# A decoder layer on one core: FFN activations transposed by DMA instead of TensorE, and the tile loop unrolled

## The chip, the cores and the metric

The kernel runs on one core of a Trainium2 chip. The metric is device time in microseconds; the median of three runs of the kernel before is 566.8 us (564.99 to 567.63). Five engines work side by side and meet only at semaphores: TensorE (PE; its weight loads are shown as PEld), VectorE (DVE), ScalarE (ACT), GpSimd (POOL) and SyncE (SP), which issues the DMAs here.

## The reference

One pre-norm decoder layer on x [4, 1024, 256], in three residual parts. The first is a gated linear recurrence along the sequence; the second is cross-attention with 16 heads on 64 context rows and one null key; the third is a quantized FFN of width 1024. The change touches the third:

```python
def _act_quant(x):
    scale = 127.0 / jnp.clip(jnp.max(jnp.abs(x), axis=-1, keepdims=True), 1e-05)
    xq = jnp.clip(jnp.round(x * scale), -128.0, 127.0) / scale
    return x + jax.lax.stop_gradient(xq - x)
def _bitlinear(x, w):
    return jnp.einsum('bsi,oi->bso', _act_quant(x), _weight_quant(w))
gate = jax.nn.silu(_bitlinear(x, w_gate))
up = _bitlinear(x, w_up)
return _bitlinear(gate * up, w_down)

x = x + _L0_attn_ref(_layernorm(x), w_qkva, gamma)
x = x + _L0_xattn_ref(_layernorm(x), ctx_2048, Wq, Wkv, null_kv, Wout, ln_scale, ln_bias)
x = x + _L0_ffn_ref(_layernorm(x), w_gate, w_up, w_down)
```

So each row of activations is scaled by its own maximum and rounded to an integer twice: ahead of gate and up (256 values, here n), and ahead of the down product (1024 values, here h).

## The kernel before

The 4096 rows are T = 32 tiles of 128 rows. Stage 1, up to about 187 us, is the recurrence and the folding of the attention weights. Stages 2 and 3, attention and FFN, then run in one software pipeline over the tiles. Each engine has its own function `stages2_3(n, u4)`, called with n from -2 to 37, and in step n it works on different tiles at once: softmax of tile n+2, attention output of tile n, statistics of x2 for n-2, the FFN's input for n-3, hidden layer for n-5, and quantizing, transposing and down product for n-6. What runs when is set by the order in which these functions are written; an engine stands still at each wait. `tiles(...)` runs steps -2 to 7 and 28 to 37 as straight code and steps 8 to 27 as a hardware loop of four steps a pass. `late(n)` (n >= 32) picks another order in the last steps, where only the FFN is left.

The FFN of one tile, by lines of the kernel before. ScalarE normalizes (L670, `norm3`); VectorE takes the maximum (L1074) and makes scale and reciprocal (L1098, L1101, `qs` and `qr`). GpSimd multiplies and adds MAGIC, which rounds (L535), then subtracts it into bf16 (L542, `n3`). TensorE transposes n (L1332, `input_T`), ScalarE evicts it (L678, `nT3`). TensorE makes gate and up (L1120, `gate_up`), ScalarE applies silu (L662, after loading its table), and VectorE multiplies (L1003, `hidden_layer`) and takes the maximum (L1078). ScalarE scales h and adds MAGIC (L718); VectorE subtracts MAGIC into bf16 (L1047, `nh3`). TensorE transposes the eight blocks (L1383), ScalarE evicts them (L737, `nhT3`). TensorE makes the down product (L1120 with `wdT`), VectorE adds it (L1011, `residual`), and SP stores the tile (L431).

Of the attention: GpSimd makes p (L495, L498) from `rden` (L990, after `exp_sum`, L985). TensorE transposes p into banks 4 and 5 (L1351, L1359, and L1363 for the null part pTn). ScalarE evicts bank 4 (L709) and pTn (L712), VectorE pTn's lesser part (L1031) and bank 5 (L1036). TensorE multiplies (L1373, L1392, L1393); VectorE takes statistics (L1085, L1091); GpSimd makes scale and bias in three small instructions (L522 to L528); ScalarE applies them (L652, `norm_out`); GpSimd adds (L483 to L487). GpSimd has three like them for the FFN's norm (L509 to L515).

Of the kernel before, what the change touches and what calls it, by code (L numbers as in the profile page):

```python
# [21 lines left out]
BF16 = mybir.dt.bfloat16  # L22
ALU = mybir.AluOpType
# [9 lines left out]
def decoder_layer(nc, x, ctx_in, w_qkva, gamma, Wq, Wkv, null_kv, Wout, ln_scale, ln_bias,  # L33
# [25 lines left out]
    with ExitStack() as stack:  # L59
# [66 lines left out]
        hw = sbuf("hw", [P, 2])  # L126
# [22 lines left out]
        def carve(region, spec):  # L149
            views, at = {}, 0  # L150
            for name, n in spec:
# [12 lines left out]
                             ("nvsel", HC * NP)])  # L164
# [42 lines left out]
        nhT3 = s["nhT"].bitcast(BF16).rearrange("p (k n) -> p k n", k=FC)  # L207
# [115 lines left out]
        nT_psum = sem("nT_psum")  # L323
        nT_ready = sem("nT_ready")
# [7 lines left out]
        nhT_psum = sem("nhT_psum")  # L332
        nhT_ready = sem("nhT_ready")
# [53 lines left out]
        S23 = (-2, 8, T - 4, T + 6, 4)  # L387
# [5 lines left out]
        def _(sp):  # L393
# [42 lines left out]
        def _(pool):  # L436
# [41 lines left out]
            def stages2_3(n, u4):  # L478
# [10 lines left out]
                if exists(n + 1, T):  # L489

                    pool.wait_ge(rden_done, n + 2)
                    if positive(n):
# [8 lines left out]
                        .then_inc(p_ready, 1)  # L501
                if exists(n - 2, T):
# [27 lines left out]
                if exists(n - 3, T):  # L530
# [6 lines left out]
                    count, free = registers(pool, n - 2, n - 4)  # L537
                    pool.wait_ge(consts_set, 2)
                    pool.wait_ge(zq_done, count)
                    if positive(free):  # L540
                        pool.wait_ge(nT_psum, free)
# [3 lines left out]
            tiles(pool, stages2_3, *S23)  # L545


        @block.scalar
        def _(act):
# [123 lines left out]
            def input_T(n, u):  # L673

                act.wait_ge(nT_psum, n - 3)
                if positive(n - 5):
                    act.wait_ge(up_psum, n - 5)
                act.activation(nT3[:, u, :, :].rearrange("p k n -> p (k n)"), bank(6).bitcast(BF16)[:, 0:D],  # L678
                               ACT.Copy).then_inc(nT_ready, 1)

# [16 lines left out]
            def stages2_3(n, u4):  # L697
# [6 lines left out]
                if exists(n, T):  # L704
# [34 lines left out]
                if not late(n) and exists(n - 4, T):  # L739
                    input_T(n, u)  # L740
# [6 lines left out]

            tiles(act, stages2_3, *S23)


        @block.vector
        def _(dve):
# [240 lines left out]
            def hidden_layer(n, v):  # L993
# [4 lines left out]
                if late(n):  # L998
                    dve.wait_ge(nh_ready, n - 6)
                    dve.wait_ge(p_ready, 2 * T)  # L1000
                elif positive(n - 5):
                    dve.wait_ge(nh_ready, n - 5)
# [4 lines left out]
            def residual(n, slot):  # L1007
# [3 lines left out]
                dve.scalar_tensor_tensor(out=xs[:, n, :], in0=bank(5, D), scalar=hw[:, slot:slot + 1],  # L1011
# [3 lines left out]
            def stages2_3(n, u4):  # L1015
# [11 lines left out]
                if exists(n, T):  # L1027
# [5 lines left out]
                    dve.wait_ge(pT1_psum, n + 1)  # L1033
# [15 lines left out]
                if late(n):  # L1049
                    residual(n - 7, v)  # L1050
# [383 lines left out]
```

## Time and profile before

| | before |
|---|---|
| median of 3 runs | 566.8 us |
| lowest, highest | 564.99, 567.63 us |
| profiled execution: span | 562.9 us |
| median less that span | 3.9 us |
| busy PE, DVE, ACT, POOL | 512.4, 479.9, 349.1, 301.1 us |

The span runs from the first to the last instruction of the execution that was profiled; its own device time isn't listed apart, so sums are made against the span and 3.9 us are added. A row of an engine in order of time gives start, duration, engine, line and operation; a difference of two starts tells more than a duration, since instructions overlap at their ends. A bracket at a row's end is the time that the engine stood idle before it, and what it waited for.

### The profile page before, as it was taken

Reading aid. Unit: us, or ns where it says so; the run is one execution under the profiler, and the core shown is the slowest. Engines: PE = TensorE matmul, PEld = TensorE weight load, DVE = VectorE, ACT = ScalarE, POOL = GpSimd, SP = SyncE. Lnnn points to the kernel's source line nnn. Section 1 sums busy time; section 2 is a strip of 40 time slices with the busy share of each in tenths; the row PEclk is TensorE's granted clock in tenths of the full one; section 3 lists DMA queues with packets and bytes.
Section 4 is the critical chain, followed back from the end, with each engine's and each line's share of the span. In section 5 each row is a group of like instructions: output and inputs, shape, how many; then the busy total and the mean of one; then the engine's idle time right before and its main releaser. Section 6 shows DMA issues by size and latency. Waiting matters only on the chain. (4 is left out here: it accounts for less than half of the span.)

```text
span 562.9 us, 11113 instructions
## 1 busy us (share of the span) xinstructions
PE 512.4 (91%) x3226; PEld 419.2 (74%) x3226; DVE 479.9 (85%) x1017; ACT 349.1 (62%) x476; POOL 301.1 (53%) x451
## 2 busy tenths in 40 slices
PE   2889999998998888999999999999999999998765
PEld 1667778765787787888788888888887888885533
DVE  5899998969535767799999999999999999997884
ACT  4422341432142323578988888889889888885764
POOL 3112216500000467787777867776878677777740
PEclk9999999999999999899999999999999999999988
DMA  8991000000000000000000000000000000000001
GB/s 283 369 394 39 1 1 0 1 1 1 0 1 0 1 2 2 0 2 20 11 10 12 19 9 9 10 18 9 9 19 9 9 9 19 9 10 15 15 19 38
DMA packets 14925, 19.80 MB, mean 35 GB/s; under 512 B 1328, under 2 KB 12848, under 8 KB 14896
## 3 DMA queue, kind: packets, MB, share of 16 engines
q1 hardware_dynamic: 14896, 19.44, 9.9%
q8 instruction: 16, 0.26, 0.2%
q14 instruction: 13, 0.11, 0.1%
HBM read 15.24 MB, written 4.19 MB: 35 GB/s over the span
## 5 line engine op out<-in xcount | busy, mean ns | idle before, releaser
L495 POOL TENSOR_TENSOR region_d<-region_d,rden 128x1024 f32<-128x1024 f32 x32 | 60.9, 1902 | 124.5 <-DVE rden L990 124.5
L1120 PE MATMUL psum<-Mhi,xT2hi 128*128 (+1 forms) x256 | 74.8, 292 | 1.9 <-DVE xT2lo L947 1.6
L1120 PE MATMUL psum<-Mlo,xT2hi 128*128 (+1 forms) x256 | 72.4, 283 | 0.0
L1120 PE MATMUL psum<-Mhi,xT2lo 128*128 (+1 forms) x256 | 72.3, 283 | 0.0
L1373 PE MATMUL psum<-VW,region_d 128*128 (+1 forms) x256 | 61.9, 385 | 6.3 <-DVE pTn L1031 6.3
L1392 PE MATMUL psum<-VW,region_d 128*128 (+1 forms) x256 | 62.9, 389 | 0.0
L1373 PEld LDWEIGHTS psum<-VW,region_d 128*128 128x128 f32 x256 | 48.4, 191 | 16.2 <-DVE pTn L1031 7.6
L973 DVE TENSOR_REDUCE mx<-psum 128x8 f32<-128x520 f32 x64 | 44.6, 697 | 8.0 <-PE psum L1120 5.9
L1392 PEld LDWEIGHTS psum<-VW,region_d 128*128 128x128 f32 x256 | 47.1, 193 | 5.4
L1120 PEld LDWEIGHTS psum<-Mhi,xT2hi 128*128 128x128 f32 x256 | 48.2, 188 | 3.0 <-issue 2.7
L1120 PEld LDWEIGHTS psum<-Mlo,xT2hi 128*128 128x128 f32 x256 | 48.3, 189 | 0.0
L1120 PEld LDWEIGHTS psum<-Mhi,xT2lo 128*128 128x128 f32 x256 | 48.2, 188 | 0.0
L976 DVE TENSOR_TENSOR region_d<-psum,mx 128x520 f32<-128x520 f32 x64 | 44.8, 700 | 2.2
L652 ACT ACTIVATE region_d<-psum,sc 128x256 f32<-128x256 f32 x32 | 17.8, 558 | 41.3 <-POOL sc L528 41.3
L461 POOL TENSOR_TENSOR pw_out<-pw_in,expo 128x8 f32<-128x8 f32 x8 | 13.1, 1643 | 51.4 <-DVE pw_in L784 51.4
L746 ACT ACTIVATE region_d<-region_d 128x1040 f32<-128x1040 f32 x32 | 34.3, 1073 | 9.5 <-DVE region_d L976 9.3
L985 DVE TENSOR_REDUCE den<-region_d 128x16 f32<-128x1040 f32 x32 | 39.3, 1228 | 0.2
L1003 DVE SCALAR_TENSOR_TENSOR region_c<-psum,zw,region_c 128x1024 f32<-128x1024 f32 x29 | 37.2, 1284 | 1.4 <-issue 0.6
L542 POOL TENSOR_SCALAR region_c<-region_d 128x256 bf16<-128x256 f32 x32 | 35.4, 1106 | 4.8 <-POOL region_d L535 0.3
L737 ACT ACTIVATE region_d<-psum 128x1024 bf16<-128x1024 bf16 x32 | 32.5, 1017 | 8.6 <-PE psum L1383 8.6
L561 ACT ACTIVATE region_a<-psum 128x1024 f32<-128x1024 f32 x8 | 8.2, 1028 | 47.4 <-PE psum L1136 47.4
L662 ACT ACTIVATE region_c<-psum,zw 128x1024 f32<-128x1024 f32 x32 | 35.6, 1113 | 2.6 <-PE psum L1120 2.3
(153 smaller groups left out, 1403.3 us busy)
## 6 DMA issues: line engine op xcount, KB each, us to landing
out_dram<-xs SPq DMA_DIRECT2D x32, 128.0 KB, 1.7
xs<-in_x_dram SPq DMA_DIRECT2D x1, 2560.0 KB, 16.4
VW<-in_L_xattn_Wkv_dram SPq DMA_DIRECT2D x1, 2048.0 KB, 17.2
region_b<-in_L_xattn_Wkv_dram SPq DMA_DIRECT2D x1, 2048.0 KB, 17.1
xs<-in_x_dram SPq DMA_DIRECT2D x3, 512.0 KB, 6.5
region_w<-in_L_ffn_w_gate_dram SPq DMA_DIRECT2D x1, 1024.0 KB, 10.1
region_w<-in_L_ffn_w_up_dram SPq DMA_DIRECT2D x1, 1024.0 KB, 12.5
region_w<-in_L_ffn_w_down_dram SPq DMA_DIRECT2D x1, 1024.0 KB, 16.8
```

The source lines that it names most:

```text
L495: pool.tensor_tensor(p2[:, v, 0:H * MK].rearrange("p (h j) -> p h j", j=MK), e[:, :, 0:MK], rden[:, v, :].unsqueeze(2).broadcast_to([P, H, ...
L542: pool.tensor_scalar(n3[:, v, :], z3[:, v, :], MAGIC, QMAX, ALU.subtract, ALU.min) \
L662: act.activation(sg3, banks(0, 2).rearrange("p b n -> p (b n)"), ACT.Silu, scale=zw[:, v, 0:1]).then_inc(silu_ready, 1)
L737: act.activation(nhT3.rearrange("p k n -> p (k n)"), bank(4).bitcast(BF16), ACT.Copy) \
L746: act.activation(e2[:, u, :], e2[:, u, :], ACT.Exp).then_inc(exp_done, 1)
L973: dve.tensor_reduce(mx[:, hh, :].rearrange("p (b h) -> p b h", h=HB), scores, AX.X, ALU.max) \
L976: dve.tensor_tensor(e2[:, u, hh * 2 * HB * J:(hh + 1) * 2 * HB * J].rearrange("p (b h j) -> p b h j", b=2, j=J), scores, mx[:, hh, :].rear ...
L985: dve.tensor_reduce(den[:, :], e2[:, slot, :].rearrange("p (h j) -> p h j", j=J), AX.X, ALU.add) \
L1003: dve.scalar_tensor_tensor(out=hidden(n - 5), in0=banks(2, 2).rearrange("p b n -> p (b n)"), scalar=zw[:, v, 1:2], in1=sg3, op0=ALU.mult, ...
L1120: mm = pe.matmul(dst, lhsT, rhs, start=i == 0, stop=i == len(terms) - 1)
L1373: pe.matmul(bank(7, D), pT[:, pair, :], VW[:, batch(n), pair, :], start=pair == 0, stop=False)
L1392: pe.matmul(bank(7, D), pT[:, pair, :], VW[:, batch(n), pair, :], start=False, stop=False)
```

## The change

1. All 39 steps, n from -2 to 38, are straight code on every engine; there is no loop in stages 2 and 3, and one step more.
2. ScalarE writes the scaled h as int16 (`nq3`, a buffer of its own), which rounds it. GpSimd casts int16 to bf16 (`nh3`, L526 of the changed kernel). VectorE's subtraction is gone.
3. GpSimd's `n3` is made by multiplying with 1 and adding -MAGIC, in place of subtract and minimum.
4. TensorE's transposes of n and h and ScalarE's two evictions are gone. SP issues two DMA transposes a tile, SBUF to SBUF: 128x1024 for h (L439) and 128x256 for n (L445), each with one semaphore for each of two destination buffers. `nhT3` has two buffers now, `nh3` and `nq3` one each. The stores of the output stand in the same queue.
5. The down product and `residual` are those of tile n-7 in every step. In steps 32 to 37 `residual` had n-7 before as well.
6. The eviction of bank 5 (pT's second half) goes from VectorE to ScalarE, ahead of the scaling of h and silu.

```diff
@@ SP
-            with sp.Fori(0, T) as t:
-                sp.wait_ge(x3_done, t + 1)
-                sp.dma_start(out_t[:, t, :], xs[:, t, :]).then_inc(stored, 16)
+            def stages2_3(n, u4):
+                u, v = u4 % 2, 1 - u4 % 2
+                if exists(n - 6, T):
+                    sp.wait_ge(nh_ready, n - 5)
+                    if positive(n - 7):
+                        sp.wait_ge(down_psum, n - 7)
+                    sp.dma_start_transpose(nhT3[u], nh3).then_inc(nhT_ready[u], 16)
+                if exists(n - 3, T):
+                    sp.wait_ge(n3_ready, n - 2)
+                    if positive(n - 4):
+                        sp.wait_ge(up_psum, n - 4)
+                    sp.dma_start_transpose(nT3[:, v, :, :], n3[:, v, :]).then_inc(nT_ready[v], 16)
+                if exists(n - 7, T):
+                    sp.wait_ge(x3_done, n - 6)
+                    sp.dma_start(out_t[:, n - 7, :], xs[:, n - 7, :]).then_inc(stored, 16)
@@ GpSimd, between p and the three small instructions
+                if exists(n - 6, T):
+                    pool.wait_ge(hq_done, n - 5)
+                    if positive(n - 6):
+                        pool.wait_ge(nhT_ready[v], 16 * ((n - 7) // 2 + 1))
+                    pool.tensor_copy(nh3, nq3).then_inc(nh_ready, 1)
...
-                    pool.tensor_scalar(n3[:, v, :], z3[:, v, :], MAGIC, QMAX, ALU.subtract, ALU.min) \
+                    pool.tensor_scalar(n3[:, v, :], z3[:, v, :], 1.0, -MAGIC, ALU.mult, ALU.add) \
@@ ScalarE
+                    act.wait_ge(pT1_psum, n + 1)
+                    act.activation(pT[:, HC // 2:HC, :], bank(5).rearrange("p (c n) -> p c n", n=P), ACT.Copy) \
+                        .then_inc(pT1_ready, 1)
...
-                    act.activation(hidden(n - 6), hidden(n - 6), ACT.Identity, bias=MAGIC, scale=qr[:, u, 0:1]) \
-                        .then_inc(hq_done, 1)
+                    if positive(n - 6):
+                        act.wait_ge(nh_ready, n - 6)
+                    act.activation(nq3, hidden(n - 6), ACT.Copy, scale=qr[:, u, 0:1]).then_inc(hq_done, 1)
...
-                if late(n) and exists(n - 4, T):
-                    input_T(n, u)
-                if exists(n - 6, T):
-                    act.wait_ge(nhT_psum, n - 5)
-                    if positive(n - 6):
-                        act.wait_ge(down_psum, n - 6)
-                    act.activation(nhT3.rearrange("p k n -> p (k n)"), bank(4).bitcast(BF16), ACT.Copy) \
-                        .then_inc(nhT_ready, 1)
@@ VectorE
-                    dve.tensor_copy(pT[:, HC // 2:HC, :], bank(5).rearrange("p (c n) -> p c n", n=P)) \
-                        .then_inc(pT1_ready, 1)
...
-                    dve.tensor_scalar(nh3, hidden(n - 6), MAGIC, QMAX, ALU.subtract, ALU.min) \
-                        .then_inc(nh_ready, 1)
                 if late(n):
-                    residual(n - 7, v)
+                    residual(n - 7)
...
-                if exists(n - 6, T) and not (isinstance(n, int) and T - 1 <= n < T + 5):
-                    residual(n - 6, u)
+                if exists(n - 7, T) and not late(n):
+                    residual(n - 7)
@@ TensorE
-                if exists(n - 6, T):
-                    pe.wait_ge(nh_ready, n - 5)
...
-                    for k in range(FC):
-                        mm = pe.transpose(bank(4).bitcast(BF16)[:, k * P:(k + 1) * P], nh3[:, k * P:(k + 1) * P],
-                                          ident16[:, :])
...
-                if exists(n - 6, T):
-                    pe.wait_ge(nhT_ready, n - 5)
+                if exists(n - 7, T):
+                    pe.wait_ge(nhT_ready[v], 16 * ((n - 7) // 2 + 1))
                     pe.wait_ge(pT1_ready, upto(n + 1, T))
-                    group(bank(5, D), [(nhT3[:, k, :], wdT[:, k, :]) for k in range(FC)]) \
+                    group(bank(5, D), [(nhT3[v][:, k, :], wdT[:, k, :]) for k in range(FC)]) \
```

TensorE's order in an odd step, from the attention product on, before; `ident` is the identity of a transpose, `VW` the attention output's weights, and region_d holds pT, n's and h's transposes:

```order
L1373 MATMUL psum<-VW,region_d 128x256 [waits pT0_ready,pTn_ready]
L1373 MATMUL psum<-VW,region_d 128x256 x3
L1383 MATMUL psum<-ident,region_d 128x128 [waits nhT_ready,pT0_ready,nh_ready]
L1383 MATMUL psum<-ident,region_d 128x128 x7
L1332 MATMUL psum<-ident,region_c 128x128 [waits nT_ready,xT2_lo_ready,n3_ready]
L1332 MATMUL psum<-ident,region_c 128x128
L1392 MATMUL psum<-VW,region_d 128x256 [waits pT1_ready]
L1392 MATMUL psum<-VW,region_d 128x256 x3
L1393 MATMUL psum<-VWnull,pTn 128x256
L1120 MATMUL psum<-wdT,region_d 128x256 [waits x3_done,pT1_ready,nhT_ready]
L1120 MATMUL psum<-wdT,region_d 128x256 x7
```

And in the changed kernel:

```order
L1357 MATMUL psum<-VW,region_d 128x256 [waits pT0_ready,pTn_ready]
L1357 MATMUL psum<-VW,region_d 128x256 x3
L1362 MATMUL psum<-VW,region_d 128x256 [waits pT1_ready]
L1362 MATMUL psum<-VW,region_d 128x256 x3
L1363 MATMUL psum<-VWnull,pTn 128x256
L1116 MATMUL psum<-wdT,region_d 128x256 [waits x3_done,pT1_ready,nhT_ready0]
L1116 MATMUL psum<-wdT,region_d 128x256 x7
```

The ten transposes between the two halves of the attention product are gone, and the down product is that of a tile earlier.

TensorE's order in the tail, before, from the down product of step 31 over step 32 (`wgT` is gate, `wuT` up, `wdT` down):

```order
L1120 MATMUL psum<-wdT,region_d 128x256 [waits x3_done,pT1_ready,nhT_ready]
L1120 MATMUL psum<-wdT,region_d 128x256 x7
L1332 MATMUL psum<-ident,region_c 128x128 [waits nT_ready,xT2_lo_ready,n3_ready]
L1332 MATMUL psum<-ident,region_c 128x128
L1383 MATMUL psum<-ident,region_d 128x128 [waits nhT_ready,pT0_ready,nh_ready]
L1383 MATMUL psum<-ident,region_d 128x128 x7
L1120 MATMUL psum<-wgT,region_d 128x512 [waits silu_ready,sim_sub,nT_ready]
L1120 MATMUL psum<-wgT,region_d 128x512 x3
L1120 MATMUL psum<-wuT,region_d 128x512 [waits h_ready,sim_sub]
L1120 MATMUL psum<-wuT,region_d 128x512 x3
L1120 MATMUL psum<-wdT,region_d 128x256 [waits x3_done,pT1_ready,nhT_ready]
L1120 MATMUL psum<-wdT,region_d 128x256 x7
```

And in the changed kernel, steps 31 and 32:

```order
L1116 MATMUL psum<-wgT,region_d 128x512 [waits silu_ready,sim_sub,nT_ready1]
L1116 MATMUL psum<-wgT,region_d 128x512 x3
L1116 MATMUL psum<-wuT,region_d 128x512 [waits h_ready,sim_sub]
L1116 MATMUL psum<-wuT,region_d 128x512 x3
L1116 MATMUL psum<-wdT,region_d 128x256 [waits x3_done,pT1_ready,nhT_ready0]
L1116 MATMUL psum<-wdT,region_d 128x256 x7
L1116 MATMUL psum<-wgT,region_d 128x512 [waits silu_ready,sim_sub,nT_ready0]
L1116 MATMUL psum<-wgT,region_d 128x512 x3
L1116 MATMUL psum<-wuT,region_d 128x512 [waits h_ready,sim_sub]
L1116 MATMUL psum<-wuT,region_d 128x512 x3
L1116 MATMUL psum<-wdT,region_c 128x256 [waits x3_done,pT1_ready,nhT_ready1]
L1116 MATMUL psum<-wdT,region_c 128x256 x7
```

Gate and up stay ahead of the down product, but it is the one that VectorE's `residual` wants in the same step, where before that one had been made a step earlier; and gate now waits for the DMA of n (`nT_ready`).

SyncE's queue in two steps of the changed kernel; before, it held the store alone:

```order
L439 DMA_TRANSPOSE region_c<-region_d 128x8x128 [waits down_psum,nh_ready]
L445 DMA_TRANSPOSE region_d<-region_c 128x2x128 [waits up_psum,n3_ready]
L448 DMA out_dram<-xs 128x256 [waits x3_done]
L439 DMA_TRANSPOSE region_d<-region_d 128x8x128 [waits down_psum,nh_ready]
L445 DMA_TRANSPOSE region_d<-region_c 128x2x128 [waits up_psum,n3_ready]
L448 DMA out_dram<-xs 128x256 [waits x3_done]
```

Each step's queue is now h's transpose, n's transpose, the store, each with its own wait.

## Rows read from the trace of the kernel before

**Rows 1.** TensorE in order of time: start, us, engine, line, operation
```profile
306.74 0.47 PE L1393 MATMUL psum<-VWnull,pTn 80*128 80x256 f32 x1
...
317.42 0.47 PE L1393 MATMUL psum<-VWnull,pTn 80*128 80x256 f32 x1
...
328.97 0.47 PE L1393 MATMUL psum<-VWnull,pTn 80*128 80x256 f32 x1
...
337.47 0.61 PE L1383 MATMUL psum<-ident,region_d 128*128 128x128 bf16 x8
...
338.03 1.95 PE L1392 MATMUL psum<-VW,region_d 128*128 x8
339.63 0.47 PE L1393 MATMUL psum<-VWnull,pTn 80*128 80x256 f32 x1
```

**Rows 2.** busy us by window: PE, PEld, DVE, ACT, POOL, clock, DMA, GB/s
```profile
250.00:500.00 250.00, 246.81 (x1760) 210.44 (x1759) 239.42 (x486) 215.75 (x281) 185.85 (x296) 1.00 0.04 12
537.00:541.00 4.00, 3.84 (x18) 2.08 (x19) 2.17 (x7) 2.36 (x3) 2.73 (x6) 0.57 0.10 33
```

**Rows 3.** VectorE in order of time, one tile of the steady loop
```profile
335.02 0.69 DVE L1036 COPY region_d<-psum 128x512 f32<-128x512 f32 x1
335.74 0.69 DVE L1047 TENSOR_SCALAR region_d<-region_c 128x1024 bf16<-128x1024 f32 x1
336.35 1.23 DVE L985 TENSOR_REDUCE den<-region_d 128x16 f32<-128x1040 f32 x1
...
338.21 1.28 DVE L1003 SCALAR_TENSOR_TENSOR region_c<-psum,zw,region_c 128x1024 f32<-128x1024 f32 x1
...
341.39 0.18 DVE L1091 BATCH_NORM_AGGREGATE mv<-st 128x2 f32<-128x6 f32 x1
```

**Rows 4.** groups by line, the eviction of h's transposes: busy, mean ns
```profile
L737 ACT ACTIVATE region_d<-psum 128x1024 bf16<-128x1024 bf16 x32 | 32.5, 1017 | 8.6 <-PE psum L1383 8.6
```

**Rows 5.** ScalarE in order of time, the same tile
```profile
332.56 0.56 ACT L652 ACTIVATE region_d<-psum,sc 128x256 f32<-128x256 f32 x1 [1.42 <-POOL sc L528]
...
333.68 0.60 ACT L709 ACTIVATE region_d<-psum 128x512 f32<-128x512 f32 x1
```

**Rows 6.** GpSimd in order of time, the same tile
```profile
338.15 1.90 POOL L495 TENSOR_TENSOR region_d<-region_d,rden 128x1024 f32<-128x1024 f32 x1 [1.13 <-DVE rden L990]
...
341.88 0.22 POOL L522 TENSOR_SCALAR sc<-mv 128x1 f32<-128x1 f32 x1
...
342.91 0.27 POOL L528 TENSOR_SCALAR sc<-mv,sc 128x1 f32<-128x1 f32 x1 [0.17 <-POOL sc L524]
```

**Rows 7.** groups by line, GpSimd's instructions with one large input
```profile
L542 POOL TENSOR_SCALAR region_c<-region_d 128x256 bf16<-128x256 f32 x32 | 35.4, 1106 | 4.8 <-POOL region_d L535 0.3
...
L535 POOL TENSOR_SCALAR region_d<-region_d,qr 128x256 f32<-128x256 f32 x32 | 15.3, 479 | 5.4 <-DVE qr L1101 5.4
...
L452 POOL TENSOR_SCALAR region_w<-region_w,wrecip 128x2048 f32<-128x2048 f32 x3 | 6.0, 1990 | 0.0
```

**Rows 8.** DMA issues: KB each, median us to landing
```profile
out_dram<-xs SPq DMA_DIRECT2D x32, 128.0 KB, 1.7
...
gcol<-in_L_attn_gamma_dram SPq DMA_DIRECT2D x1, 1.0 KB, 5.5
```

**Rows 9.** TensorE in order of time, the tail
```profile
538.09 1.91 PE L1120 MATMUL psum<-wgT,region_d 128*128 128x512 bf16 x4
...
543.74 1.03 PE L1120 MATMUL psum<-wgT,region_d 128*128 128x512 bf16 x4
...
545.47 1.04 PE L1120 MATMUL psum<-wdT,region_d 128*128 128x256 bf16 x8
```

**Rows 10.** VectorE in order of time, the tail
```profile
527.95 0.17 DVE L1101 RECIPROCAL qr<-qs 128x2 f32<-128x2 f32 x1
...
530.75 0.47 DVE L1011 SCALAR_TENSOR_TENSOR xs<-psum,hw,xs 128x256 f32<-128x256 f32 x1
...
533.59 0.17 DVE L1101 RECIPROCAL qr<-qs 128x2 f32<-128x2 f32 x1
...
549.86 0.17 DVE L1101 RECIPROCAL qr<-qs 128x1 f32<-128x1 f32 x1
```

More of the change, by code:

```diff
@@ L22 @@
 BF16 = mybir.dt.bfloat16
+I16 = mybir.dt.int16
 ALU = mybir.AluOpType
@@ L206, in decoder_layer @@
         h3 = [c["h"], s["e"][:, 0:FI]]
-        nhT3 = s["nhT"].bitcast(BF16).rearrange("p (k n) -> p k n", k=FC)
+        nhT3 = [r["nhT"].bitcast(BF16).rearrange("p (k n) -> p k n", k=FC) for r in (s, c)]
+        nq3 = c["nq"].bitcast(I16)
         x_loaded = [sem(f"x_loaded{i}") for i in range(4)]
@@ L322, in decoder_layer @@
         n3_ready = sem("n3_ready")
-        nT_psum = sem("nT_psum")
-        nT_ready = sem("nT_ready")
+        nT_ready = [sem(f"nT_ready{i}") for i in range(2)]
         gate_psum = sem("gate_psum")
@@ L331, in decoder_layer @@
         nh_ready = sem("nh_ready")
-        nhT_psum = sem("nhT_psum")
-        nhT_ready = sem("nhT_ready")
+        nhT_ready = [sem(f"nhT_ready{i}") for i in range(2)]
         down_psum = sem("down_psum")
@@ L386, in decoder_layer, with steps @@
         S1 = (-2, 2, NG - 2, NG + 1, 2)
-        S23 = (-2, 8, T - 4, T + 6, 4)
+        def steps(step):
+            for n in range(-2, T + 7):
+                step(n, n % 4)
         block = stack.enter_context(nc.Block())
@@ L536, in stages2_3 @@
                         .then_inc(zq_done, 1)
[L537 to L541, printed above, removed]
-                    pool.tensor_scalar(n3[:, v, :], z3[:, v, :], MAGIC, QMAX, ALU.subtract, ALU.min) \
+                    pool.wait_ge(zq_done, n - 2)
+                    if positive(n - 4):
+                        pool.wait_ge(nT_ready[v], 16 * ((n - 3) // 2))
+                    pool.tensor_scalar(n3[:, v, :], z3[:, v, :], 1.0, -MAGIC, ALU.mult, ALU.add) \
                         .then_inc(n3_ready, 1)
-            tiles(pool, stages2_3, *S23)
+            steps(stages2_3)
         @block.scalar
@@ L746, in stages2_3 @@
                     act.activation(e2[:, u, :], e2[:, u, :], ACT.Exp).then_inc(exp_done, 1)
-            tiles(act, stages2_3, *S23)
+            steps(stages2_3)
         @block.vector
@@ L1005, in hidden_layer, with residual @@
                     .then_inc(h_ready, 1)
-            def residual(n, slot):
+            def residual(n):
                 dve.wait_ge(hw_done, n + 1)
                 dve.wait_ge(down_psum, n + 1)
-                dve.scalar_tensor_tensor(out=xs[:, n, :], in0=bank(5, D), scalar=hw[:, slot:slot + 1],
+                dve.scalar_tensor_tensor(out=xs[:, n, :], in0=bank(5, D), scalar=hw[:, n % 4:n % 4 + 1],
                                          in1=xs[:, n, :], op0=ALU.mult, op1=ALU.add) \
@@ L1105, in stages2_3 @@
                 if exists(n - 5, T):
-                    dve.tensor_scalar(hw[:, v:v + 1], qs[:, v, 0:1], wscale[:, 2:3], None, ALU.mult) \
+                    dve.tensor_scalar(hw[:, (n - 5) % 4:(n - 5) % 4 + 1], qs[:, v, 0:1], wscale[:, 2:3], None, ALU.mult) \
                         .then_inc(hw_done, 1)
-                if exists(n - 6, T) and not (isinstance(n, int) and T - 1 <= n < T + 5):
-                    residual(n - 6, u)
-            tiles(dve, stages2_3, *S23)
+                if exists(n - 7, T) and not late(n):
+                    residual(n - 7)
+            steps(stages2_3)
         @block.tensor
@@ L1323, in gate_up @@
                 mm.then_inc(up_psum, 1)
-            def input_T(n, u):
-                pe.wait_ge(n3_ready, n - 3)
-                pe.wait_ge(xT2_lo_ready, upto(half(n) + 2 + u, T // 2))
-                if positive(n - 4):
-                    pe.wait_ge(nT_ready, n - 4)
-                for k in range(KD):
-                    mm = pe.transpose(bank(6).bitcast(BF16)[:, k * P:(k + 1) * P], n3[:, u, k * P:(k + 1) * P], ident16[:, :])
-                mm.then_inc(nT_psum, 1)
             def stages2_3(n, u4):
@@ L1399, in stages2_3 @@
                     gate_up(n + 1, u)
[L1400 to L1402 removed]
+                if exists(n - 7, T):
+                    pe.wait_ge(nhT_ready[v], 16 * ((n - 7) // 2 + 1))
                     pe.wait_ge(pT1_ready, upto(n + 1, T))
[L1404 to L1406 removed]
+                    if positive(n - 7):
+                        pe.wait_ge(x3_done, n - 7)
+                    group(bank(5, D), [(nhT3[v][:, k, :], wdT[:, k, :]) for k in range(FC)]) \
                         .then_inc(down_psum, 1)
[L1409 removed]
+            steps(stages2_3)
 _INS = ['x', 'ctx_2048', 'L0_attn_w_qkva', 'L0_attn_gamma', 'L0_xattn_Wq', 'L0_xattn_Wkv', 'L0_xattn_null_kv',
```

45 lines of the change are left out of this document (8 added, 37 removed).

## The prediction, made before the changed kernel ran

> **What bounds the kernel now.** I read four views in this order. First, how often a tile leaves the loop: the last product of the attention output (L1393) is one instruction a tile, and from 306.74 to 328.97 two tiles take 22.23 us, from 317.42 to 339.63 again 22.21, so 11.1 us a tile [rows 1]. The loop's body is four tiles, and the step from 306.74 to 317.42 crosses its back edge while that from 328.97 to 339.63 does not: 10.68 against 10.66, so the branch is free. Second, who is busy between 250 and 500: TensorE 246.8 and VectorE 239.4 of 250 us, GpSimd 185.9 [rows 2]. Two engines are full at once. Third, the order inside one tile on each engine, to find the loop of waits that appears when VectorE is relieved. Fourth, the last 35 us, where only the FFN is left and every instruction waits for another engine.
>
> **The steady loop: what is taken away.** TensorE loses eight transposes of h and two of n: 337.47 to 338.03, 0.56 us [rows 1]. VectorE loses the copy of pT's second half, 0.72 (335.02 to 335.74), and the quantizing of h, 0.61 (335.74 to 336.35) [rows 3]. ScalarE loses an eviction of 1.02 [rows 4] and a small one, and takes the pT copy, whose first half costs it 0.60 [rows 5]. If TensorE alone set the pace the loop would run at 11.1 - 0.56 = 10.55. VectorE alone would run at 11.1 - 1.33 = 9.8.
>
> **What is late next.** Two loops of waits are shorter than 11.1 today and do not show. (a) VectorE from hidden_layer to the statistics of the output: 338.21 to 341.39 + 0.18 = 3.36 [rows 3]; GpSimd's three small instructions that make scale and bias: 341.88 to 342.91 + 0.27 = 1.30 [rows 6]; ScalarE from norm_out to the end of silu, read as 332.56 to the next hidden_layer at 338.21, less 0.15 for VectorE's own work, 5.50 [rows 3, 5]; about 0.1 for hand-offs. That is 10.3 today. The change puts the pT copy (0.6) in front of silu: 10.9. (b) Over two tiles: VectorE's whole work of a tile (9.7), GpSimd from p to scale and bias (338.15 to 341.88, 3.73 [rows 6]) plus the new cast, plus 1.30, plus ScalarE's 6.1: 20.9 + cast, so 11.0 a tile with a cast of 1.1. So the period goes from 11.1 to about 10.9, not to 10.55. In 22 tiles (6 to 27) that is -4.6 us; the ends are 0 and 22 x 0.56 = -12.3. For the six tiles ahead of the FFN I take nothing.
>
> **The cast on GpSimd.** No row shows int16 to bf16. Two rows of one plain input give 1990 ns for 2048 elements and 479 for 256, so 0.84 ns an element and 1.13 us for 1024; the quantizer with bf16 output takes 1106 for 256, and with the same fixed part 3.6 us for 1024 [rows 7]. Whether its bf16 output or its operations (subtract, minimum) make it slow no row tells. I take 1.13, nearest to the row with one plain pass, and keep 3.6 for the rivals. The quantizer of n becomes the multiply and add of the fast row: up to -0.6 on GpSimd, which isn't the pace.
>
> **The transposes by DMA.** The trace has none. The nearest rows: a store of 128 KB in long pieces lands after 1.7 us, a 1 KB load in 4-byte pieces after 5.5 [rows 8]. A transpose is made of small pieces, and one of h carries four times what one of n does. I take T = 2.5 for n and 4 for h, with 1.7 to 5.5 and 1.7 to 9 as ends. In the steady loop this is covered: h's is issued when GpSimd's cast ends and wanted by the down product one step later, some 11 us on, and by the next cast, which overwrites its only source, some 9.5 us on; n's is wanted after more than a step. SP's queue is in order (h, n, store), and each waits for what comes later in the tile than the one before it, so the new waits hold nobody up while both land within a period. The cover ends at h's transpose + cast = 10.9.
>
> The Trainium skill, "DMA: Bandwidth & Descriptors", section "Anatomy of one DMA", fits 2.0 us + bytes / 436 GB/s, for the gpsimd path. As an estimate from that page n's 64 KB would take 2.15 and h's 256 KB 2.6, and the sum below would be 3 us shorter (584); no row here shows it.
>
> **The tail.** Here nothing covers them. In the order of before, residual(n-7) on VectorE waits for a down product of the previous TensorE step. In the changed order it waits for the down product of the same step, which stands behind gate_up(n+1), which waits for n's DMA transpose, which waits for GpSimd's n3, which waits for qr, which VectorE makes after the previous residual. So in steps 32 to 35 one loop goes through all of them: qr and hand-off 0.3, GpSimd twice 0.48 and a gap of 0.1 [rows 7], T, hand-offs 0.3, gate_up 1.73 (543.74 to 545.47), down 1.04 [rows 9], residual to the next qr 2.84 (530.75 to 533.59) [rows 10]: 7.3 + T. The first costs 1.0 more, since GpSimd is still at its three small instructions, and the last two lack the statistics and n's maximum, some 1.5 together. Four of them: 28.7 + 4T, where before qr at 527.95 and at 549.86 are 21.9 apart [rows 10]. Excess 6.8 + 4T. Behind that, one quantizing (0.6) is gone, and the last tile has cast and DMA (1.1 + h's) in place of quantizing, PE transposes and eviction (0.6 + 0.45 + 1.02 and a hand-off): h's transpose - 1.6. Sum 5.2 + 4 x 2.5 + 4 = +19.2, ends +13.7 and +36.
>
> **The clock.** In the tail of before, where waits of some microseconds lie between its products, TensorE's granted clock was 0.57 of full from 537 to 541, that is mostly 1.2 instead of 2.4 GHz [rows 2], and the four gate products from 538.09 took 1.91 us where those from 543.74 took 1.03 [rows 9]. In the changed tail TensorE works 2.8 us of 10 in each of these steps; at the low level each costs up to 2.8 more, 12 in all. I take half, +6.
>
> **Sum**, against the profiled execution: 562.9 - 4.6 + 19.2 + 6 = 583.5. The median of the runs shown lies 3.9 above that span: 587.
>
> **Unrolling** I cost at nothing, by the two steps above. The Trainium skill, "Runtime: NRT & Kernel Launch", section "Instruction fetch mechanics", says that a taken branch whose target isn't in the fetched window stalls until a DMA has brought it, and that kernels prefer unrolling for it. By that rule, with a fetch as long as the 1.7 us store, the loop's few back edges would give back some 8 us (579); the 10.68 beside 10.66 speaks against it.
>
> **Rivals.** (1) Faster: the end of the loop of waits is loose, the steady tiles reach TensorE's 10.55 (-12.3) and lose the last short waits too (-3), VectorE's lost copy is won in the six early tiles (0.72 each, -4.3), and the transposes land in 1.7 (+13.7): 557, or 561 as a median. It decides when steady and early tiles together give over 14 us. For it: VectorE is really relieved; against: loops (a) and (b). Halfway to it, with a tail at its lower end and no clock loss, lies 566, no change. (2) The cast takes 3.6: a loop from p (3.73) through cast, scale and bias (1.30), norm_out to pTn (2.0), pTn's lesser part (0.4), then exp_sum to the next p, 336.35 to 338.15 = 1.8 [rows 3, 6], is 9.3 + cast, so 12.9 a tile: 1.8 x 26 = +47, with the tail 638. (3) The single buffer of quantized h: if its transpose takes 12 us instead of 4, the loop is cast + transpose = 13.2, +2.1 x 26 = +55, and a longer tail: 650 and more. (4) The tail's loop isn't there, because the transposes are issued far ahead. Then the tail costs h's transpose alone and the sum is 565. The order speaks against it.
>
> **Chances.** The forecast 0.70 (572 to 612 by its ends), (1) 0.05, no change by halfway or by (4) 0.07, (2) 0.09, (3) 0.09. The range 565 to 612 leaves out (1), (2) and (3), with the edges 2 in 10. Faster by over 0.5% (about what a measurement of this kernel can tell from no change) 0.06, within 0.07, slower 0.87.
>
> **What would show it.** L1363 (L1393 of before) 10.9 us apart in the middle, with VectorE waiting for silu; casts of 1.1; DMA transposes landing in 2 to 5 us; in the last 55 us gate_up waiting for a DMA four times, residual waiting for TensorE, and qr some 9.8 apart; granted clock well under full there. A middle at 10.5 or a tail as short as before would make it wrong.

## The result and the profile after

The changed kernel takes 581.2 us (median of 4 runs, 580.2 to 582.5), the kernel before 565.9 us in the same session (4 runs, 564.9 to 567.6): 1.026 times as long, with a 95% interval from 1.023 to 1.029. The profiled execution spans 578.4 us where that of before spans 562.9, so the two traces differ by 15.5 us and the medians by 15.3: the traces hold the whole difference.

The top of the page of the changed kernel:

```profile
span 578.4 us, 9250 instructions
PE 501.0 (87%) x2878; PEld 402.0 (70%) x2906; DVE 434.2 (75%) x953; ACT 321.9 (56%) x444; POOL 305.3 (53%) x483
PEclk9989999999999999999999999999999999897676
DMA packets 57949, 30.49 MB, mean 53 GB/s; under 512 B 44336, under 2 KB 55856, under 8 KB 57904
```

The steady loop first, as in [rows 1]: TensorE in order of time, the last attention product of each tile. It stands at L1363 now.

```profile
192.76 0.47 PE L1363 MATMUL psum<-VWnull,pTn 80*128 80x256 f32 x1
...
258.52 0.47 PE L1363 MATMUL psum<-VWnull,pTn 80*128 80x256 f32 x1
269.03 0.47 PE L1363 MATMUL psum<-VWnull,pTn 80*128 80x256 f32 x1
...
475.16 0.47 PE L1363 MATMUL psum<-VWnull,pTn 80*128 80x256 f32 x1
...
516.74 0.47 PE L1363 MATMUL psum<-VWnull,pTn 80*128 80x256 f32 x1
```

The 20 tiles between 258.52 and 475.16 take 10.83 us each. Before, the same 20 (from 262.26 to 484.48) took 11.11 each. The last tile leaves the loop at 516.74; before it did at 526.07. So the loop did become faster, by 9.3 us, and the change loses all of it and 15.5 more behind it: from the last L1363 to the end lie 61.7 us, where before lay 36.8. The tail is 24.8 us longer.

In the tail, VectorE in order of time, as in [rows 10] (L1019 is residual, L1097 makes qr):

```profile
519.21 0.17 DVE L1097 RECIPROCAL qr<-qs 128x2 f32<-128x2 f32 x1
...
528.28 0.48 DVE L1019 SCALAR_TENSOR_TENSOR xs<-psum,hw,xs 128x256 f32<-128x256 f32 x1 [6.67 <-PE psum L1116]
531.13 0.17 DVE L1097 RECIPROCAL qr<-qs 128x2 f32<-128x2 f32 x1
540.20 0.48 DVE L1019 SCALAR_TENSOR_TENSOR xs<-psum,hw,xs 128x256 f32<-128x256 f32 x1 [7.48 <-PE psum L1116]
543.04 0.17 DVE L1097 RECIPROCAL qr<-qs 128x2 f32<-128x2 f32 x1
...
563.98 0.16 DVE L1097 RECIPROCAL qr<-qs 128x1 f32<-128x1 f32 x1
```

TensorE there, as in [rows 9]:

```profile
524.43 1.49 PE L1116 MATMUL psum<-wgT,region_d 128*128 128x512 bf16 x3 [4.60 <-DMA region_d<-region_c]
527.14 1.04 PE L1116 MATMUL psum<-wdT,region_c 128*128 128x256 bf16 x8
...
534.79 1.89 PE L1116 MATMUL psum<-wgT,region_d 128*128 128x512 bf16 x4 [6.62 <-DMA region_d<-region_c]
...
538.18 1.92 PE L1116 MATMUL psum<-wdT,region_d 128*128 128x256 bf16 x8
```

and GpSimd with the last instruction ahead of n's transpose, and the transpose on SP's queue:

```profile
531.46 0.48 POOL L560 TENSOR_SCALAR region_d<-region_d,qr 128x256 f32<-128x256 f32 x1 [0.60 <-DVE qr L1097]
532.03 0.41 POOL L565 TENSOR_SCALAR region_c<-region_d 128x256 bf16<-128x256 f32 x1
```
```profile
532.46 1.17 SPq L445 DMA_TRANSPOSE region_d<-region_c  x1
```

One turn of the tail's loop can be added up from these rows, qr at 531.13 to qr at 543.04: 0.33 to GpSimd's start; 0.98 there, to 532.44; 2.35 to the gate product at 534.79, which is the DMA transpose with both hand-offs; 3.39 for gate and up, to 538.18; 2.02 for down and its hand-off, to 540.20; 2.84 from residual to the next qr. That is 11.91 us, with no gap left over. The four turns take 11.9, 11.9, 10.8 and 10.2. In each TensorE stands idle for 4.6 to 6.6 us and VectorE for 6.7 to 7.5, each for the other's end of the turn. The waits grouped over the tail, 520 to 578 us (total, times, longest), say it in two lines:

```profile
DVE xs L1019 <- PE psum L1116: 35.8, 7, 7.5
...
PE psum L1116 <- DMA region_d<-region_c: 23.9, 4, 6.6
```

### The profile page after: what moved, and what is told of

The parts are those of the page before. It is cut to its first block, busy times and chain, and to the rows that moved or that the text cites. A ratio compares the mean times of both kernels' runs of the same rounds, so it can differ in the third digit from the quotient of the medians.

```text
span 578.4 us, 9250 instructions
## 1 busy us (share of the span) xinstructions
PE 501.0 (87%) x2878; PEld 402.0 (70%) x2906; DVE 434.2 (75%) x953; ACT 321.9 (56%) x444; POOL 305.3 (53%) x483
## 2 busy tenths in 40 slices
DMA packets 57949, 30.49 MB, mean 53 GB/s; under 512 B 44336, under 2 KB 55856, under 8 KB 57904
## 4 chain that ended last, share of the span: by engine, by line
DVE 23%; PE 22%; issue 18%; POOL 18%; ACT 12%; DMA 4%; DVEq 1%; POOLq 1%; SPq 0%; ACTq 0%
PE psum L1116 15%; DVE amax L1074 4%; DVE region_c L1011 4%; ACT L685 4%; PE psum L1132 3%; ACT region_c L685 3%; POOL sc L549 3%; DVE region_a L861 2%; POOL region_d L526 2%; POOL xs L506 2%; POOL region_d L504 2%; DMA region_d<-region_c 2%; POOL region_d L502 2%; ACT region_d L693 1%; POOL region_d L560 1%
## 5 line engine op out<-in xcount | busy, mean ns | idle before, releaser
L1116 PE MATMUL psum<-Mhi,xT2hi 128*128 128x260 f32 x256 | 74.8, 292 | 1.9 <-DVE xT2lo L955 1.6
L1116 PE MATMUL psum<-Mlo,xT2hi 128*128 128x260 f32 x256 | 72.4, 283 | 0.0
L1116 PE MATMUL psum<-Mhi,xT2lo 128*128 128x260 f32 x256 | 72.3, 282 | 0.0
L1357 PE MATMUL psum<-VW,region_d 128*128 128x256 f32 x256 | 62.6, 389 | 6.0 <-DVE pTn L1039 6.0
L1362 PE MATMUL psum<-VW,region_d 128*128 128x256 f32 x256 | 60.7, 380 | 0.0
L1357 PEld LDWEIGHTS psum<-VW,region_d 128*128 128x128 f32 x256 | 49.0, 193 | 16.2 <-DVE pTn L1039 7.3
L1116 PE MATMUL psum<-wgT,region_d 128*128 128x512 bf16 x100 | 30.0, 413 | 28.5 <-DMA region_d<-region_c 23.9
L1362 PEld LDWEIGHTS psum<-VW,region_d 128*128 128x128 f32 x256 | 48.9, 191 | 6.8
L984 DVE TENSOR_TENSOR region_d<-psum,mx 128x520 f32<-128x520 f32 x64 | 44.8, 700 | 2.2
L1019 DVE SCALAR_TENSOR_TENSOR xs<-psum,hw,xs 128x256 f32<-128x256 f32 x32 | 15.3, 477 | 35.8 <-PE psum L1116 35.8
L526 POOL CAST region_d<-region_c 128x1024 bf16<-128x1024 int16 x32 | 33.1, 1036 | 12.7 <-ACT region_c L738 9.1
L1116 PE MATMUL psum<-wuT,region_d 128*128 128x512 bf16 x128 | 36.3, 410 | 3.8 <-DVE region_d L984 3.8
```

The lines of the kernel that those rows point to most:

```text
L526: pool.tensor_copy(nh3, nq3).then_inc(nh_ready, 1)
L984: dve.tensor_tensor(e2[:, u, hh * 2 * HB * J:(hh + 1) * 2 * HB * J].rearrange("p (b h j) -> p b h j", b=2, j=J), scores, mx[:, hh, :].rear ...
L1116: mm = pe.matmul(dst, lhsT, rhs, start=i == 0, stop=i == len(terms) - 1)
L1357: pe.matmul(bank(7, D), pT[:, pair, :], VW[:, batch(n), pair, :], start=pair == 0, stop=False)
L1362: pe.matmul(bank(7, D), pT[:, pair, :], VW[:, batch(n), pair, :], start=False, stop=False)
```

## Experiments

Every experiment starts from the changed kernel unless said otherwise. Each was timed in three rounds against the kernel before on the same chip; ratios are to that kernel, so they can be compared across sessions.

### The tail's loop: put the down product first

In the tail alone TensorE does the down product of tile n-7 ahead of gate_up(n+1), so that residual no longer waits for a product that stands behind n's transpose. Both products are still there, and so are all the transposes.

```diff
-                if isinstance(n, int) and n >= T - 1 and exists(n - 4, T):
+                if n == T - 1:
                     gate_up(n + 1, u)
...
                         .then_inc(down_psum, 1)
+                if late(n) and exists(n - 4, T):
+                    gate_up(n + 1, u)
```

> The changed kernel with one edit: in steps 32 to 35 TensorE makes the down product ahead of gate and up. Theory A (the tail's loop runs through all engines because residual stands behind gate and the DMA of n): the loop is opened, the four steps from qr of step 31 to qr of step 35 shrink from 44.8 us to 20 to 26, TensorE's clock in the tail is higher, and the median goes from 581 to 557 to 563. Rival B (the tail is long because DMA transposes and a slow clock are slow in any order): the order matters little, those four steps stay above 38 us, and the median stays above 575. The middle of the kernel stays at 10.8 us a tile in both.

Measured: 560.6 us (560.1 to 561.8), ratio 0.990 (0.988 to 0.992). The order of two products on one engine was worth 3.5% of the kernel and turned the loss into a gain. VectorE's qr in the tail:

```profile
519.69 0.17 DVE L1097 RECIPROCAL qr<-qs 128x2 f32<-128x2 f32 x1
...
525.48 0.17 DVE L1097 RECIPROCAL qr<-qs 128x2 f32<-128x2 f32 x1
...
533.39 0.17 DVE L1097 RECIPROCAL qr<-qs 128x2 f32<-128x2 f32 x1
...
537.41 0.17 DVE L1097 RECIPROCAL qr<-qs 128x2 f32<-128x2 f32 x1
...
543.64 0.16 DVE L1097 RECIPROCAL qr<-qs 128x1 f32<-128x1 f32 x1
```

Four turns take 23.95 us where they took 44.8 (519.21 to 563.98) in the changed kernel and 21.9 before [rows 10]. The tail behind the last L1363 is 41.3 us instead of 61.7. With all the transposes by DMA still there the tail is 4.5 us longer than before, not 24.8: most of its length came from the loop through them. Part of the gain is clock: 0.84 was granted from 530 to 550 us where the changed kernel has 0.59, and what the low clock costs there is measured below, at about 7 us. The steady loop is untouched, 10.84.

### Unrolling alone

The kernel before, with its loop of four-tile bodies written out and nothing else changed (shown for TensorE; the same for VectorE, ScalarE and GpSimd; SyncE's loop over the stores stays).

```diff
-            tiles(pe, stages2_3, *S23)
+            for n_ in range(-2, T + 6):
+                stages2_3(n_, n_ % 4)
```

> The kernel before with its loop over the tiles written out, and nothing else. Theory A (the loop's back edge costs nothing, as 10.68 us over it beside 10.66 without it showed): within 0.3% of the kernel before, 11.1 us a tile. Rival B (a taken branch stalls for instructions): 3 to 8 us faster. Rival C (more instructions have to be brought in, and cost time): slower by over 1.5 us.

Measured: 566.3 us, ratio 0.999 (0.997 to 1.000). The loop's back edge cost nothing that these runs can tell. The Trainium skill, "Runtime: NRT & Kernel Launch", section "Instruction fetch mechanics", has a taken branch out of the fetched window stall for a fetch. Priced at a store's 1.7 us, the prediction's estimate was that 8 us would come back. The measurement bounds it at 0.3% of the time, 1.7 us. No run here shows whether the start of this loop lay outside the window, so it prices this loop and doesn't test the rule.

### The cast twice

GpSimd writes each cast once into a scratch buffer and then again where it is used.

```diff
+                    pool.tensor_copy(nvsel[:, 0:512].bitcast(BF16), nq3)
                     pool.tensor_copy(nh3, nq3).then_inc(nh_ready, 1)
```

> The changed kernel with GpSimd's cast made twice a tile, the first time into memory that is free at that time: 1.04 us more on GpSimd between p and scale and bias. Theory A (loop (b) of the prediction, over two tiles and through the cast, is the one that sets the period): 0.5 us more a tile, 11.3 to 11.4, and 12 to 15 us in all, 593 to 597. Rival B (loop (a), without the cast, sets it, and (b) has 0.3 us or more to spare): under 0.3 us a tile, under 590. Rival C (GpSimd's own work sets it): 1.04 a tile, over 603.

Measured: 593.7 us (593.1 to 594.2), ratio 1.047. The groups by line (busy, mean ns):

```profile
L527 POOL CAST region_d<-region_c 128x1024 bf16<-128x1024 int16 x32 | 33.3, 1040 | 0.0
L526 POOL CAST region_c<-region_c 128x1024 bf16<-128x1024 int16 x32 | 33.1, 1036 | 11.4 <-ACT region_c L739 7.8 <-DMA region_d<-region_d 3.2
```

GpSimd was busy for only 192.8 of the 250 us from 250 to 500 in the changed kernel, and still a cast of 1.04 us more lengthens each steady tile by 0.49, to 11.32: GpSimd stands on a loop of waits. A two-tile loop (b) pays half of the added cast, 0.52. A one-tile loop with a slack of about half a microsecond (rival 2's, 9.3 + casts = 11.38) would land in the same place. The run shows that with more than one cast's time a loop through the cast sets the pace; it doesn't tell those two apart, nor does it show that this loop already did so with one cast.

### The copy of pT back to VectorE

The changed kernel moved the copy of pT's second half from VectorE to ScalarE, where it stands ahead of silu in loop (a). Here it goes back.

```diff
-                    act.wait_ge(pT1_psum, n + 1)
-                    act.activation(pT[:, HC // 2:HC, :], bank(5).rearrange("p (c n) -> p c n", n=P), ACT.Copy) \
-                        .then_inc(pT1_ready, 1)
...
+                    dve.wait_ge(pT1_psum, n + 1)
+                    if positive(n):
+                        dve.wait_ge(out_psum, n)
+                    dve.tensor_copy(pT[:, HC // 2:HC, :], bank(5).rearrange("p (c n) -> p c n", n=P)) \
+                        .then_inc(pT1_ready, 1)
```

> The changed kernel with the eviction of pT's second half given back to VectorE, as in the kernel before. Theory A (the period is set by the loop through ScalarE, VectorE and GpSimd in which this copy stands ahead of silu): that loop gets 0.6 us shorter, VectorE has 10.4 to 10.5 us of work a tile, so the period falls by 0.1 to 0.3 us, 576 to 580. Rival B (two-tile loop (b) sets it; there the copy only moves from one of its engines to another): unchanged period, 10.8 to 11.0, 580 to 585.

Measured: 586.7 us (584.4 to 588.9), ratio 1.034 (1.030 to 1.038): slower than the changed kernel, and outside both expectations. The waits between 255 and 520 us, first in the changed kernel, then with the copy on VectorE:

```profile
ACT region_d L675 <- POOL sc L553: 45.8, 24, 5.1
DVE region_c L1011 <- ACT region_c L685: 34.6, 25, 1.9
POOL region_d L514 <- DVE rden L998: 28.8, 24, 1.8
```
```profile
ACT region_d L675 <- POOL sc L553: 60.7, 25, 5.5
POOL region_d L514 <- DVE rden L995: 38.1, 24, 1.9
DVE region_c L1008 <- ACT region_c L685: 12.1, 24, 0.7
```

VectorE's wait for silu did fall, from 34.6 to 12.1 us, as loop (a) says. But GpSimd now waits longer for rden and ScalarE for scale and bias. The copy stands on VectorE between pTn's lesser part and exp_sum, and that place is on another loop: p (3.73 to the small instructions), cast 1.04, scale and bias 1.30, norm_out to pTn 2.0, the lesser part 0.4, exp_sum to the next p 1.8. This is 10.3 us today and 11.0 with the copy of 0.72 in it; measured, a steady tile takes 10.94. That is an account and not a proof: the trace has VectorE wait for pTn in 11 of its tiles (8.7 us; 2 times and 4.6 us in the changed kernel), while in the others VectorE's own work reaches up to that place. I had this loop in the prediction, as rival 2's, and left it out when I expected this run. Against the changed kernel the steady 20 tiles cost 2.2 us, the six ahead of the FFN 3.1, the last four of the loop 2.6.

### Keeping TensorE busy in the tail

Products whose result nobody reads stand ahead of each late gate_up, so that TensorE has no long idle stretch. The order is the changed kernel's.

```diff
+            def busy(k):
+                for i in range(k):
+                    pe.matmul(bank(6), wgT[:, 0, 0:P], wgT[:, 0, 0:512], start=i == 0, stop=i == k - 1)
...
+                    if late(n):
+                        busy(24)
                     gate_up(n + 1, u)
+                if n in (T + 5, T + 6):
+                    busy({T + 5: 20, T + 6: 10}[n])
```

> The changed kernel with spare products on TensorE (into a bank that nobody reads) in the waits of steps 32 to 35, 37 and 38: 24, 20 and 10 of 512 columns, all ahead of the waits for the DMA. The order of the real work is unchanged. Theory A (part of the tail is the low clock, which comes from TensorE standing still): granted clock near 1.00 in the tail, gate, up and down together 2.8 us instead of 4.3 to 5.3, the steps of 11.9, 11.9, 10.8 and 10.2 shrink to 9.9 to 10.2 or below, 6 to 9 us less in all, 572 to 575. Rival B (the low clock costs nothing since DMA and hand-offs set the step): less than 2 us.

Measured: 574.2 us (572.5 to 575.6), ratio 1.013 (1.009 to 1.017). The windows (busy us of PE, PEld, DVE, ACT, POOL, then granted clock, DMA share, GB/s) of 530 to 550 us, the changed kernel first, the filled one second:

```profile
530.00:550.00 20.00, 8.58 (x24) 3.41 (x25) 6.78 (x16) 5.51 (x6) 5.58 (x11) 0.59 0.22 47
```
```profile
530.00:550.00 20.00, 17.12 (x87) 8.23 (x86) 9.60 (x22) 5.51 (x6) 5.96 (x12) 1.00 0.21 47
```

TensorE was busy for 8.6 of 20 us at a granted clock of 0.59, so mostly at 1.2 GHz; with work that means nothing it was busy for 17.1 and ran at 2.4 GHz throughout. Its gate, up and down of a step are back at 2.8 us. The four turns take 38.0 us instead of 44.8:

```profile
520.50 0.17 DVE L1097 RECIPROCAL qr<-qs 128x2 f32<-128x2 f32 x1
...
558.49 0.17 DVE L1097 RECIPROCAL qr<-qs 128x1 f32<-128x1 f32 x1
```

So the low clock cost the changed kernel about 7 us (1.3% by the ratios, 6.8 in the turns).

### n of the last four tiles by TensorE

Only the n of tiles 28 to 31 goes back to transposes by TensorE and an eviction by ScalarE. The order stays as changed, gate_up ahead of down.

```diff
-                if exists(n - 3, T):
+                if exists(n - 3, T - 4):
...
+            def input_T(n, u):
+                pe.wait_ge(n3_ready, n - 3)
+                for k in range(KD):
+                    mm = pe.transpose(bank(6).bitcast(BF16)[:, k * P:(k + 1) * P], n3[:, u, k * P:(k + 1) * P], ident16[:, :])
+                mm.then_inc(nTt_psum, 1)
```

> The changed kernel with n of the last four tiles transposed by TensorE and evicted by ScalarE as before, the order of gate and down as changed. Theory A (each of the four tail steps holds n's whole transpose once): from the end of n3 to gate 0.9 to 1.1 us instead of 2.8, so 1.7 to 1.9 us less in each of four steps, 7 to 8 in all and somewhat more if the clock rises; 571 to 575. Rival B (the order alone makes the tail long, the transpose's time is hidden behind something else): less than 3 us.

Measured: 574.1 us (573.1 to 575.5), ratio 1.014. TensorE in the tail:

```profile
529.93 0.27 PE L1322 MATMUL psum<-ident,region_c 128*128 128x128 bf16 x2 [4.40 <-POOL region_c L569]
530.68 1.89 PE L1129 MATMUL psum<-wgT,region_d 128*128 128x512 bf16 x4 [0.47 <-ACT region_d L704]
```

The four turns take 37.5 us (qr at 519.36 to 556.90), 1.8 less each: the gate product starts 0.75 us after n's transposes do, where the way by DMA took 2.4 to 2.8. From the same start, then, a faster way of n gives 7 us, and getting the down product out from behind it gives 20. Both figures hold what the clock gives back with them.

### ScalarE's norm3 behind silu

In the steady loop norm3(n), which isn't urgent, moves from ahead of pT's copies and silu to behind them; loop (a) should lose its 0.4 to 0.5 us.

```diff
-                if not late(n) and exists(n - 3, T):
-                    norm3(n, v)
...
                     silu_gate(n, v)
+                if not late(n) and exists(n - 3, T):
+                    norm3(n, v)
```

> The changed kernel with ScalarE's normalizing for the FFN (norm3, 0.5 to 0.6 us) moved behind silu in the steps of the middle. Theory A (the period is set by the loops from rden or hidden_layer over GpSimd and norm_out, in which norm3 stands between norm_out and pT and pTn): 0.3 to 0.5 us less a tile, 10.83 to 10.4 or 10.5, where TensorE's own work stops it; 573 to 577 in all. Rival B (TensorE already sets the period): no change in the period, 580 to 582.

Measured: 576.4 us (574.2 to 578.2), ratio 1.016. The total is where it was expected, but not for the reason given: the steady 20 tiles (258.81 to 473.69) take 10.74 each, 0.09 less, where 0.3 to 0.5 had been expected. From the first to the last L1363 the trace saves 3.9 us, of which the 20 tiles hold 1.8 and the last four 1.2. Either the two-tile loop (b) or VectorE's own waits hold the period at 10.7; which of them is open. TensorE leaves little behind them: it is busy for 244.6 of the 250 us from 250 to 500 here, against 240.3 in the changed kernel, so for 10.5 of each 10.74.

### The two orders together, and n by TensorE on top

First down ahead of gate_up in the tail and norm3 behind silu, both edits as above; then the same with the n of tiles 28 to 31 by TensorE.

> Both edits: the down product first in the tail, and norm3 behind silu in the middle. If the two act in different stretches their gains add up: 560.6 less what norm3 later brings alone, 552 to 556. If they don't, 559 to 561.

> The kernel with down first and norm3 later, and in its tail the n of the last four tiles transposed by TensorE with one eviction by ACT, as in the run of that edit alone. Theory A (hand-offs of n still stand on the path when the down product goes first): in the run with down first the gate_up product waited 0.5 to 1.9 us for the transpose of n after the down product, 4.3 us over four steps; 0.9 us from n3 to its transposed form instead of 2.3 to 2.8 takes at most that, so 3 to 4 us off the 557.0 of the run with both orders: 553 to 554. Theory B (the tail is now set by the chain cast, transposes of h, down, residual, and TensorE's own work between): the shorter way of n only lengthens the wait for h (2.4 to 3.8 us at the last two), and the four transposes and the eviction stand on TensorE and ACT as new work of 0.8 us a step: 556 to 559.

Measured: 557.0 us (555.6 to 557.8), ratio 0.982 (0.979 to 0.986), for the two orders: 1.8% faster than the kernel before and 4.3% faster than the changed one. The median is 1 us above the range for gains that add up; the product of the two single ratios, each against the changed kernel, gives 0.980, so by the ratios they add up within the uncertainty. With n by TensorE on top 555.0 us (554.0 to 558.0), ratio 0.984 (0.979 to 0.988). In microseconds it looks 2 faster, between the ranges of both theories, but the kernel before was 2.3 us faster on that chip as well; by the ratios there is no difference. In the two traces the tail behind the last mark is 2.2 us shorter (38.0 against 40.2), so a small gain isn't excluded; the 3 to 4 us of theory A are not there. TensorE in the tail of the run with all three:

```profile
524.71 1.05 PE L1129 MATMUL psum<-wdT,region_d 128*128 128x256 bf16 x8 [3.17 <-DMA region_d<-region_d]
526.35 1.04 PE L1129 MATMUL psum<-wgT,region_d 128*128 128x512 bf16 x4 [0.48 <-ACT region_d L704]
...
534.29 1.05 PE L1129 MATMUL psum<-wdT,region_d 128*128 128x256 bf16 x8 [1.48 <-DMA region_d<-region_d]
...
543.37 1.32 PE L1129 MATMUL psum<-wdT,region_d 128*128 128x256 bf16 x8 [3.81 <-DMA region_d<-region_d]
```

The long waits are for h's transposes now. n's way was worth 7 us while it stood in the loop, and within the uncertainty of nothing once the down product no longer waited behind it. That is theory B's mechanism, shown by the waits more than by the time.

## Why the prediction was right

Forecast were 587 us and slower; measured 581.2, and the mechanism named was the one found: the tail's loop through all engines, closed by residual standing behind gate and the DMA of n. Exchanging the two products opened it and took 20 us away. The difference of the two spans, part by part, with L1363 (L1393 of before) as the mark between parts:

| part | predicted | measured |
|---|---|---|
| up to the first mark | 0 | +0.6 |
| six early tiles | 0 | -3.8 |
| steady tiles up to the 28th | -4.6 | -6.1 |
| last four of the loop | no term | 0.0 |
| tail, waits and transposes | +19.2 | +17.8 |
| tail, clock | +6 | +7 |
| sum | +20.6 | +15.5 |

The 3.9 us from the span to the median came out as 2.8.

**The tail** is right in its structure and, with +24.8 against +25.2, in its size. The four turns hold 22.9 of it; at the full clock they were forecast at 28.7 + 4 x 2.5 = 38.7 us, and the run with a filled tail has 38.0. That run also splits the sum: of 24.8 some 7 were clock. The split is rough, since those 7 are counted against a full clock, and the kernel before had 0.91 and not 1.00 from 530 to 550 us; what that cost it no run shows. That the low clock would cost time followed from [rows 2, 9]. That +6 came so near was luck: it was half of 12, with no reason for the half. The turn's parts came out as T and hand-offs 2.35 to 2.78 (priced 2.8), gate and up 1.73 at the full clock and 3.39 at the low one, residual to qr 2.84 as in [rows 10]. h's transpose landed sooner than priced:

```profile
region_d<-region_c SPq DMA_TRANSPOSE x32, 2.3
region_d<-region_d SPq DMA_TRANSPOSE x16, 3.1
```

These are medians from issue to landing, of n (first row) and of h (second), against 2.5 and 4. The fit quoted in the prediction (the Trainium skill, "DMA: Bandwidth & Descriptors", section "Anatomy of one DMA"), which the page states for DMAs issued by GpSimd and not by SyncE, gave 2.15 and 2.6 as estimates: near for n, half a microsecond short for h.

**The steady loop** was forecast at 10.9 us a tile and took 10.83. TensorE alone would have allowed 10.55, and that this wasn't reached is what loops (a) and (b) said: the changed kernel's VectorE waits 34.6 us for silu in the middle, a wait that isn't among those of before there. The term still came out 1.5 short, since -0.2 a tile was taken and -0.29 came. By the account of the run with the copy on VectorE the third loop, kept for rival 2 alone, lies within about half a microsecond of the other two. Three loops that close together would explain why neither edit that was meant to shorten one of them gave what it promised; that they do isn't shown.

**The early tiles** are the step that failed, by 3.8 of the 5.1 us of the sum's miss. I took nothing for them and gave no reason, though rival 1 had a price for them: VectorE's lost copy, 4.3 us. That copy is what most of it was. The six tiles from the first mark to the seventh take 58.3 us before, 54.5 in the changed kernel, and 57.6 in the changed kernel with this copy alone given back: 3.1 of the 3.8. But it isn't 0.72 in each tile, as rival 1 had it. One tile holds 2.6:

```profile
219.34 0.47 PE L1393 MATMUL psum<-VWnull,pTn 80*128 80x256 f32 x1
230.85 0.47 PE L1393 MATMUL psum<-VWnull,pTn 80*128 80x256 f32 x1
```
```profile
219.28 0.47 PE L1363 MATMUL psum<-VWnull,pTn 80*128 80x256 f32 x1
228.20 0.47 PE L1363 MATMUL psum<-VWnull,pTn 80*128 80x256 f32 x1
```

It takes 11.51 us before (first pair) and 8.92 in the changed kernel. Steady and early tiles together gave 9.9 us, where rival 1 needed over 14. The windows of 219 to 231 us of the two (columns as in the run with a filled tail), before first:

```profile
219.00:231.00 12.00, 10.22 (x57) 8.67 (x55) 6.89 (x16) 3.06 (x7) 10.26 (x17) 0.86 0.00 1
```
```profile
219.00:231.00 12.00, 10.86 (x76) 10.05 (x76) 8.15 (x22) 4.72 (x9) 9.93 (x20) 1.00 0.03 7
```

TensorE's granted clock dips there in the kernel before, and in the unrolled kernel before, and in the run with the copy of pT on VectorE (0.91 in 215 to 235 us in all three); in the changed kernel and the other seven it is 1.00. So the dip goes with the place of that copy, neither with the unrolling nor with the transposes. Why a copy of 0.7 us there decides it no run shows, nor how much of the 2.6 us the dip itself costs.

**The cast** was priced at 1.13 us from rows of GpSimd with plain input and measured 1.04; rival 2's 3.6 was out:

```profile
L526 POOL CAST region_d<-region_c 128x1024 bf16<-128x1024 int16 x32 | 33.1, 1036 | 12.7 <-ACT region_c L738 9.1
```

The quantizer's 1106 ns in [rows 7] had made bf16 output suspect. The same shape with multiply and add takes 0.41 us at L565, with the same output type: the operations were slow there, not the type. **Rival 3** needed a transpose of 12 us, and it took 3.1. **Rival 4** said that the tail's loop isn't there; the run with down first shows what that is worth, 20 us. **Unrolling** was costed at nothing and measured 0.999.

## What to carry over

When work is moved from a busy engine to a slower path that something else covers, look for the place where the cover ends: here the loop's 9 us of gain were real, and the last four tiles, with nothing beside them, paid them back almost three times. Write one turn of the tail as a closed loop, instruction by instruction, and ask of each neighbouring pair on an in-order engine whether the second has to stand behind the first; exchanging two products was worth 20 us. Where two or three loops of waits lie within half a microsecond of each other, expect little from relieving one; relieving all was not tried here.

## What the runs showed of the hardware

- A DMA transpose from SBUF to SBUF lands after 2.3 us for 128x256 bf16 and after 3.1 us for 128x1024, with 44336 packets under 512 bytes in the run; it lifts the DMA engines' share of the middle (250 to 500 us) from 0.04 to 0.21, and the only other transfers there, the stores, land after 1.9 us instead of 1.7 [rows 8]. The landings are medians.
- As a rule such a transpose holds SP for 1.17 us (n) or 1.23 us (h; three of them 2.0), a plain store for 0.57. With two transposes and a store a tile that is 3.0 of 10.8 us.
- On GpSimd int16 to bf16 runs at 1.04 us for 128x1024. An instruction on 128x256 with bf16 output takes 0.41 us with multiply and add and 1.11 with subtract and minimum.
- In the tail with its waits TensorE's clock fell: there it was granted 0.59 of full while busy for 8.6 of 20 us, and 1.00 while unread products filled it to 17.1. Filling it with useless products made the kernel 1.3% faster.
